# Attention denominators: eight key tiles summed by pair sums on GpSimd and accumulating DMAs, in place of four-tile sums split between GpSimd and TensorE

## The chip, the core and the metric

The kernel runs on one core of a Trainium2 chip. The metric is the device time of one execution in microseconds (us). TensorE multiplies matrices (PE; its weight loads are PEld), VectorE is DVE, ScalarE is ACT, GpSimd is POOL, and SyncE (SP) issues most DMAs.

## What is computed

One transformer block with a conditioned LayerNorm, in float32, over x of 2 x 2048 x 512 with 16 heads of 32 columns:

```python
c6 = silu(c) @ Wc + bc                       # shifts, scales and gates
xm = modulate(ln(x), sh_msa, sc_msa)
q, k, v = xm @ Wq + bq, xm @ Wk + bk, xm @ Wv + bv
w = softmax(einsum('bqhc,bkhc->bhqk', q / DH, k))
y = einsum('bhqk,bkhc->bqhc', w, v)
x = x + g_msa * (y @ Wo + bo)
x = x + g_mlp * (gelu(modulate(ln(x), sh_mlp, sc_mlp) @ W1 + b1) @ W2 + b2)
```

The softmax divides each query's sum of exp(score) * v by the sum of exp(score) over 2048 keys. The change touches only how that denominator is added up.

## The kernel before

Three stages run one after the other: `project`, `attend` (from L646) and `feed_forward`. The change lies in `attend`.

An iteration of `attend` handles 512 queries of one batch and of a group of four heads; there are 32 (`N_IT`). It walks over 16 tiles of 128 keys, and two tiles make a block, so there are 8 blocks in an iteration. For each tile and head, TensorE computes a score tile of 128 keys x 512 queries (`scores`, L1016), and ScalarE turns it into `probs` (exp, L902). Between two score products TensorE computes one product of the next iteration's scores the other way round (L999), whose maximum VectorE takes (`maximum`, L921). These maxima become a row that goes by DMA into the next iteration's query tile (`max_transpose` L1005, `as_row` L931, `load_row` L738). After each block TensorE multiplies the block before by v (`times_v`, L1026), four heads side by side in 32 columns each.

`probs` is a ring of five tiles (`RING`). A tile's slot is written again only when v was multiplied and the tile's sums were read (`slot_free`, L884).

The denominators are built by fours of tiles, here called quads: 128 of them, four in an iteration. GpSimd adds tile to tile: for two of the four heads it adds all four tiles up (`high_first` L812, then `high_more` L819 twice); for the other two heads it adds only tiles 0+1 and 2+3 (`low` L804, twice). That makes five GpSimd instructions of 128 x 1024 for a quad. TensorE then sums over the 128 keys of the partitions with a matrix of ones (`sums`, L1032), due after every second block (`due_quad`). As the halves of neighbouring quads are arranged, an even quad takes 4 of these matmuls and an odd one 8. ScalarE copies each result out of PSUM (`take_sum`, L850). Four heads' matmuls of 32 columns run side by side and are called a group below. In the last iteration VectorE does the `low` sums (`last_low`, L959), as it has no maxima left.

The four sums of an iteration go to `d_small` by small DMAs (L862), are added and inverted on VectorE (L938, L942), go to DRAM and come back broadcast over the partitions (L868, L874), and GpSimd multiplies `y_buf` by them (L825). The result is stored (L882). All of this happens in the iteration behind.

The banks of the maxima and of the sums come from one ring of four PSUM banks, dealt out in advance by `MaxRing`. Every engine runs its queue in order; GpSimd's, too: a wait there holds up all the sums behind it.

Of the kernel before, what the change touches and what calls it, by code (L numbers as in the profile page):

```python
# [11 lines left out]
P = 128  # L12
# [27 lines left out]
RING = 5  # L40
LEAD, BEFORE = 12, 3
# [571 lines left out]
def due_quad(b):  # L613

    return (b - 3) // 2 if b >= 3 and b % 2 == 1 else None


class MaxRing:
# [4 lines left out]
    def __init__(self):  # L623
        uses = []
        for i in range(N_IT):
            for s in range(N_MAX):
# [6 lines left out]
                if within == 2 * HPG - 1 and due_quad(b) is not None and due_quad(b) <= LAST_QUAD:  # L633
                    uses.append(("sum", due_quad(b)))
# [11 lines left out]
def attend(nc, sh, late, x, Wo, W1):  # L646
# [7 lines left out]
    with ExitStack() as ctx:  # L654
# [20 lines left out]
        d_raw, inv = sb("d_raw", [P, QPI, TOK]), sb("inv", [P, TOK])  # L675

        d_small, d_total = sb("d_small", [P, QPI, HPG * TOK // P]), sb("d_total", [P, HPG * TOK // P])
# [15 lines left out]
        low_ready, high_step, last_low_ready = sem("low_ready"), sem("high_step"), sem("last_low_ready")  # L693
# [8 lines left out]
        def low_heads(c):  # L702
            return slice(0, 2) if c % 2 == 0 else slice(2, 4)

        def high_heads(c):
            return slice(2, 4) if c % 2 == 0 else slice(0, 2)

        def lows(c, n):
            return (low_ready, 2 * c + n) if c < LAST_QUAD else (last_low_ready, 2 * (c - LAST_QUAD) + n)

        def low_slot_free(c, half):

            return c - 1 + half if c % 2 == 0 else c - 1
# [4 lines left out]
        def _(sp):  # L718
# [71 lines left out]
        def _(pool):  # L790
# [7 lines left out]
            def low(c, half):  # L798
                first = 4 * c + 2 * half
                hs = low_heads(c)  # L800
                if c >= 2:
                    pool.wait_ge(d_done, low_slot_free(c, half))
                pool.wait_ge(p_done, HPG * (first + 1) + hs.stop)
                pool.tensor_tensor(low_sum[:, (2 * c + half) % 4, :, :], probs[:, first % RING, hs, :],  # L804
                                   probs[:, (first + 1) % RING, hs, :], ALU.add).then_inc(low_ready, 1)

            def high_first(c):
                hs = high_heads(c)
                if c >= 2:
                    pool.wait_ge(d_done, c - 1)  # L810
# [708 lines left out]
```

## Time and profile before

| | us |
|---|---|
| median of 3 runs | 2892.97 (2891.18 to 2893.5) |
| the profiled execution | 2893.33 |
| its span in the trace | 2891.2 |
| PE busy in the span | 2827.3 (98%) |
| POOL busy | 2001.4 (69%) |
| DVE busy | 1995.1 (69%) |
| ACT busy | 1375.4 (48%) |

The shares are averages over the three stages. The attention loop takes some 1,690 us of the span, and each engine must be read in it alone. Matmuls overlap, so a matmul's duration is longer than the distance to the next one's start; what TensorE takes for a piece of work is read from the starts.

### The profile page before, as it was taken

What the parts mean: (1) busy time and instruction counts of PE and PEld (TensorE: products, weight loads), DVE (VectorE), ACT (ScalarE), POOL (GpSimd) and SP (SyncE); (2) the same over time, 40 slices, a digit from 0 to 9 for tenths busy, and PEclk for the clock granted to TensorE, in tenths of its full rate; (3) what the DMA queues carried; (4) which work ended last, traced back from release to release, by engine and by line L of the source; (5) the groups of instructions that cost most, each with busy time, mean ns of one, the idle gap of its engine ahead of it and who ended that gap; (6) DMA issues with size and microseconds to landing.
All of it is one profiled execution on the core that took longest, in us unless ns stands there. A gap on an engine that the chain in (4) does not pass through costs nothing. (4 is left out here: it accounts for less than half of the span.)

```text
span 2891.2 us, 40767 instructions
## 1 busy us (share of the span) xinstructions
PE 2827.3 (98%) x14713; PEld 1811.5 (63%) x14713; DVE 1995.1 (69%) x3320; ACT 1375.4 (48%) x2599; POOL 2001.4 (69%) x1015
## 2 busy tenths in 40 slices
PE   7999999999999999999999999999699999999998
PEld 5777755555555555555555555553488888888887
DVE  5556677777777777777777777773657656666754
ACT  2322266666666666666666666666311211221211
POOL 1000099999999999999999999997555555555453
PEclk9999999999999999999999999999799999999999
DMA  6555533414314314323323324302201101100000
GB/s 233 193 185 172 170 86 82 110 32 103 89 34 100 89 44 101 81 63 87 75 67 89 84 61 94 77 20 100 95 15 44 44 1 44 44 16 29 30 15 15
DMA packets 152767, 225.19 MB, mean 78 GB/s; under 512 B 31804, under 2 KB 48760, under 8 KB 152568
## 3 DMA queue, kind: packets, MB, share of 16 engines
q1 hardware_dynamic: 123036, 204.81, 25.9%
q10 hardware_dynamic: 29532, 17.79, 2.1%
q8 instruction: 118, 1.93, 0.3%
q14 instruction: 81, 0.66, 0.1%
HBM read 162.30 MB, written 58.97 MB: 77 GB/s over the span
## 5 line engine op out<-in xcount | busy, mean ns | idle before, releaser
L921 DVE TENSOR_REDUCE part_max<-m_bank 128x1 f32<-128x512 f32 x1972 | 1207.5, 681 | 385.2 <-PE m_bank L999 385.1
L902 ACT ACTIVATE probs<-s_bank 128x512 f32<-128x512 f32 x2048 | 1035.3, 626 | 196.4 <-PE s_bank L1016 192.3
L804 POOL TENSOR_TENSOR low_sum<-probs 128x1024 f32<-128x1024 f32 x248 | 588.4, 2382 | 80.4 <-ACT probs L902 80.3
L819 POOL TENSOR_TENSOR high_sum<-high_sum,probs 128x1024 f32<-128x1024 f32 x256 | 608.6, 2378 | 40.6 <-ACT probs L902 3.8
L1026 PE MATMUL y_bank<-probs,vs 128*32 128x512 f32 x4096 | 495.6, 602 | 0.0
L1395 ACT ACTIVATE h<-up_bank,vecs 128x512 f32<-128x512 f32 x128 | 88.0, 688 | 574.7 <-PE up_bank L1423 574.7
L1016 PE MATMUL s_bank<-qs,ks 97*128 97x512 f32 x768 | 317.9, 417 | 1.8 <-ACT probs L902 1.5
L1016 PE MATMUL s_bank<-late_parts,ks 97*128 97x512 f32 x768 | 319.0, 416 | 0.2 <-ACT probs L902 0.2
L812 POOL TENSOR_TENSOR high_sum<-probs 128x1024 f32<-128x1024 f32 x128 | 307.5, 2402 | 13.6 <-ACT probs L902 13.3
L1026 PEld LDWEIGHTS y_bank<-probs,vs 128*32 128x32 f32 x4096 | 107.3, 109 | 243.3 <-issue 134.3
L1016 PEld LDWEIGHTS s_bank<-qs,ks 97*128 97x128 f32 x768 | 144.4, 189 | 133.0 <-issue 78.0
L850 ACT ACTIVATE d_raw<-m_bank 128x512 f32<-128x512 f32 x124 | 74.2, 598 | 322.3 <-PE m_bank L1032 322.3
L1016 PEld LDWEIGHTS s_bank<-late_parts,ks 97*128 97x128 f32 x768 | 144.6, 188 | 123.2 <-issue 80.5
L1209 POOL TENSOR_TENSOR w_lo<-space_plain,w_hi 128x512 fp32r<-128x512 f32 x64 | 88.1, 1377 | 179.4 <-DVE w_hi L1291 179.4
L1421 PE MATMUL up_bank<-xm_hi,w_hi 128*128 128x512 f32 x512 | 206.4, 403 | 2.8 <-DVE xm_lo L1287 2.8
L1301 DVE CAST h_hi<-h 128x512 fp32r<-128x512 f32 x128 | 74.4, 582 | 190.5 <-ACT h L1395 190.5
L1423 PE MATMUL up_bank<-xm_hi,w_lo 128*128 128x512 f32 x512 | 203.6, 398 | 0.0
L1422 PE MATMUL up_bank<-xm_lo,w_hi 128*128 128x512 f32 x512 | 203.3, 397 | 0.0
L1422 PE MATMUL acc_bank<-w_lo,h_hi 128*128 128x512 f32 x512 | 202.5, 396 | 0.0
L999 PE MATMUL m_bank<-late_parts 96*128 96x512 f32 x512 | 202.5, 395 | 0.0
L1421 PE MATMUL acc_bank<-w_hi,h_hi 128*128 128x512 f32 x512 | 202.3, 395 | 0.1
L1423 PE MATMUL acc_bank<-w_hi,h_lo 128*128 128x512 f32 x512 | 202.3, 395 | 0.0
(167 smaller groups left out, 4689.3 us busy)
## 6 DMA issues: line engine op xcount, KB each, us to landing
late_parts<-q_parts SPq DMA_DIRECT2D x96, 256.0 KB, 4.8
late_parts<-k_parts SPq DMA_DIRECT2D x72, 256.0 KB, 4.6
ks<-k_parts SPq DMA_DIRECT2D x72, 256.0 KB, 5.0
late_plain<-in_x SPq DMA_DIRECT2D x16, 1024.0 KB, 7.5
q_parts<-qk_out SPq DMA_DIRECT2D x32, 512.0 KB, 3.5
k_parts<-qk_out SPq DMA_DIRECT2D x32, 512.0 KB, 3.5
space_parts<-q_parts SPq DMA_DIRECT2D x48, 256.0 KB, 5.0
space_parts<-k_parts SPq DMA_DIRECT2D x48, 256.0 KB, 4.5
```

The source lines that it names most:

```text
L804: pool.tensor_tensor(low_sum[:, (2 * c + half) % 4, :, :], probs[:, first % RING, hs, :], probs[:, (first + 1) % RING, hs, :], ALU.add).th ...
L812: pool.tensor_tensor(high_sum[:, c % 2, :, :], probs[:, 4 * c % RING, hs, :], probs[:, (4 * c + 1) % RING, hs, :], ALU.add).then_inc(high_ ...
L819: pool.tensor_tensor(high_sum[:, c % 2, :, :], high_sum[:, c % 2, :, :], probs[:, (4 * c + r) % RING, hs, :], ALU.add).then_inc(high_step, 1)
L902: act.activation(probs[:, tile % RING, h, :], s_bank[(HPG * tile + h) % 3][:, :], ACT.Exp).then_inc(p_done, 1)
L921: v.tensor_reduce(part_max[:, i % 2, hs, c:c + 1], m_bank[ring.bank["max", i, n]][:, :], AX.X, ALU.max).then_inc(m_taken, 1)
L999: pe.matmul(m_bank[ring.bank["max", i, n]][:, :], qm[i % 2][0:STACK, h, s * P:(s + 1) * P], km[c][0:STACK, h, :], start=True, stop=True).t ...
L1016: pe.matmul(s_bank[n % 3][:, :], ks[c][0:STACK + 1, h, s * P:(s + 1) * P], qs[i % 2][0:STACK + 1, h, :], start=True, stop=True).then_inc(s ...
L1026: last = pe.matmul(y_bank[h * DH:(h + 1) * DH, :], vs[:, t, h * DH:(h + 1) * DH], probs[:, tile % RING, h, :], start=(t == 0), stop=(t == ...
L1209: pool.tensor_tensor(w1_lo[:, j % 2, :, :], w1_raw[j * 4 // MT][:, :, j % (MT // 4) * P:(j % (MT // 4) + 1) * P], w1_hi[:, j % 2, :, :].bi ...
L1421: pe.matmul(bank, hi_l, hi_r, start=first, stop=False)
L1422: pe.matmul(bank, hi_l, lo_r, start=False, stop=False)
L1423: return pe.matmul(bank, lo_l, hi_r, start=False, stop=last)
```

## The change

Sums are made over eight tiles, here called a half (two halves an iteration). In a quad, GpSimd adds tiles 0+1 into `first_home(c)` and 2+3 into `second_home(c)`, for all four heads in two instructions of 128 x 1024 each. Then GpSimd issues a DMA that adds the second (1 MB) onto the first (`fold_quad`), and after each two quads one that adds one quad onto the other (`fold_half`, 1 MB). TensorE takes 4 matmuls for a half, due after every fourth block, the fifth behind the block that holds the half's last tiles. `fold_half` waits on GpSimd's queue for the DMA of the quad just before; it stands behind the next quad's `first_pair`. `second_pair` waits for the fold two quads back, and the even quads' `first_pair` for TensorE's sums of two halves back. The last four quads are not folded: TensorE takes 8 matmuls for each.

`Wo` is loaded in the last iteration, since its place serves as the second buffer. The denominators' way (move, invert, store, load, multiply, store) is spread over two iterations with two `y_buf` buffers, two moves in place of four, and other places in the queues of ScalarE, VectorE and GpSimd. The last but one iteration's result is finished after the last one's tiles. The size of the memory for GpSimd's DMA descriptors is set to 1024.

```diff
-def due_quad(b):
-
-    return (b - 3) // 2 if b >= 3 and b % 2 == 1 else None
+def due_sum(b):
+
+
+
+
+
+    if b >= N_BLOCKS - 3:
+        return LAST_HALF + b - (N_BLOCKS - 3)
+    return (b - 8) // 4 if b >= 8 and b % 4 == 0 else None
...
-        low_sum = sb("low_sum", [P, 4, 2, TOK])
-        high_sum = sb("high_sum", [P, 2, 2, TOK])
+        first_sum = sb("first_sum", [P, 4, HPG, TOK])
+        second_sum = [sb("second_sum", [P, HPG, TOK]), late.wo]
         part_max, neg_max, neg_max_row = late.part_max, late.neg_max, late.neg_max_row
-        y_buf = sb("y_buf", [P, TOK])
...
+        def first_home(c):
+            return first_sum[:, (0, 1, 2, 0)[c - LAST_QUAD] if c >= LAST_QUAD else c % 4, :, :]
+
+        def second_home(c):
+            if c >= LAST_QUAD:
+                return (second_sum[0][:, :, :], first_sum[:, 3, :, :], second_sum[0][:, :, :], first_sum[:, 1, :, :])[c - LAST_QUAD]
+            return second_sum[c % 2][:, :, :]
+
+        def firsts(c):
+            return (first_ready, 2 * c + 2) if c < LAST_QUAD else (last_first_ready, 2 * (c - LAST_QUAD) + 2)
+
+        def quad_done(c):
+            return quad_folded[c % 2], 16 * (c // 2 + 1)
...
-            sp.dma_start(late.wo[:, :, :], Wo.rearrange("(t p) n -> p t n", p=P)).then_inc(wo_in, 16)
             for i in range(N_IT - 1):
                 iteration(i)
+
+            sp.wait_ge(*quad_done(LAST_QUAD - 1))
+            sp.dma_start(late.wo[:, :, :], Wo.rearrange("(t p) n -> p t n", p=P)).then_inc(wo_in, 16)
...
+            def first_pair(c):
+                h = c // 2
+                if h >= 2 and c % 2 == 0:
+                    pool.wait_ge(d_done, h - 1)
+                if h >= 2 and c % 2 == 1:
+                    pool.wait_ge(half_folded, 16 * (h - 1))
+                for hs in PAIR:
+                    pool.wait_ge(p_done, HPG * (4 * c + 1) + hs.stop)
+                    pool.tensor_tensor(first_home(c)[:, hs, :], probs[:, 4 * c % RING, hs, :],
+                                       probs[:, (4 * c + 1) % RING, hs, :], ALU.add).then_inc(first_ready, 1)
+
+            def second_pair(c):
+                q = c - LAST_QUAD
+                if q == 1:
+                    pool.wait_ge(half_folded, 16 * LAST_HALF)
+                elif q > 1:
+                    pool.wait_ge(d_done, LAST_HALF + q - 1)
+                elif c >= 2:
+                    pool.wait_ge(*quad_done(c - 2))
+                for hs in PAIR:
+                    pool.wait_ge(p_done, HPG * (4 * c + 3) + hs.stop)
+                    pool.tensor_tensor(second_home(c)[:, hs, :], probs[:, (4 * c + 2) % RING, hs, :],
+                                       probs[:, (4 * c + 3) % RING, hs, :], ALU.add).then_inc(second_ready, 1)
+
+            def accumulate(onto, what):
+                return pool.dma_start(onto.rearrange("p h n -> p (h n)"), what.rearrange("p h n -> p (h n)"), accum_op=ALU.add)
+
+            def fold_quad(c):
+                pool.wait_ge(first_ready, 2 * c + 2)
+                pool.wait_ge(second_ready, 2 * c + 2)
+                accumulate(first_home(c), second_home(c)).then_inc(quad_folded[c % 2], 16)
+
+            def fold_half(h):
+                pool.wait_ge(*quad_done(2 * h))
+                pool.wait_ge(*quad_done(2 * h + 1))
+                accumulate(first_home(2 * h), first_home(2 * h + 1)).then_inc(half_folded, 16)
...
+                if c % QPI == QPI - 2 and c // QPI >= 2:
+                    normalise(c // QPI - 2)
                 if c < LAST_QUAD:
-                    low(c, 0)
-                high_first(c)
-                high_more(c, 2)
-                high_more(c, 3)
+                    first_pair(c)
+                if c % 2 == 0 and 0 < c <= LAST_QUAD:
+                    fold_half(c // 2 - 1)
+                second_pair(c)
                 if c < LAST_QUAD:
-                    low(c, 1)
+                    fold_quad(c)
+            normalise(N_IT - 2)
...
+                if i >= 2:
+                    act.wait_ge(y_stored, 16 * (i - 1))
...
                 act.wait_ge(av_done, tile + 1)
-                if r != 1:
-                    act.wait_ge(*lows(c, 1 + r // 2))
-                    act.wait_ge(high_step, 3 * c + max(r, 1))
+                if r == 0:
+                    act.wait_ge(*firsts(c))
+                if r == 2:
+                    act.wait_ge(second_ready, 2 * c + 2)
 
             for i in range(N_IT):
                 for t in range(NKT):
                     tile = NKT * i + t
                     if t == 2 and i:
                         take_y(i - 1)
-                    if tile >= 8 and tile % 4 == 0 and (tile - 8) // 4 < LAST_QUAD:
-                        take_sum((tile - 8) // 4)
+                    if tile >= 18 and tile % 8 == 2 and (tile - 18) // 8 < LAST_HALF:
+                        take_sum((tile - 18) // 8)
...
+                    if i >= 2:
+                        if t == 1:
+                            store_inv(i - 2)
                         if t == 5:
-                            move_sums(i - 1)
-                        if t == 8:
-                            store_inv(i - 1)
-                        if t == 10:
-                            load_inv(i - 1)
-                        if t == NKT - 1:
-                            store_y(i - 1)
+                            load_inv(i - 2)
+                        if t == 13:
+                            store_y(i - 2)
+                    if i and t == 11:
+                        move_sums(i - 1)
+            store_inv(N_IT - 2)
             take_y(N_IT - 1)
+            load_inv(N_IT - 2)
             take_last_sums()
+            store_y(N_IT - 2)
...
+            def last_first(q):
+                c = LAST_QUAD + q
+                if q % 2 == 0:
+                    v.wait_ge(d_done, LAST_HALF - 1 + q // 2)
+                elif q == 1:
+                    v.wait_ge(half_folded, 16 * (LAST_HALF - 1))
+                else:
+                    v.wait_ge(d_done, LAST_HALF + 1)
+                for hs in PAIR:
+                    v.wait_ge(p_done, HPG * (4 * c + 1) + hs.stop)
+                    v.tensor_tensor(first_home(c)[:, hs, :], probs[:, 4 * c % RING, hs, :],
+                                    probs[:, (4 * c + 1) % RING, hs, :], ALU.add).then_inc(last_first_ready, 1)
...
+                        if i and n == INVERT_AT:
+                            invert_small(i - 1)
+            invert_small(N_IT - 3)
...
+            def sums(u):
+                if u <= LAST_HALF:
+                    bank_free(("sum", u))
+                if u < LAST_HALF:
+                    pe.wait_ge(half_folded, 16 * (u + 1))
+                    for h in range(HPG):
+                        last = add_up(u, h, first_home(2 * u)[:, h, :], True, True)
                 else:
+                    c = LAST_QUAD + u - LAST_HALF
+                    pe.wait_ge(*firsts(c))
+                    for h in range(HPG):
+                        add_up(u, h, first_home(c)[:, h, :], c == LAST_QUAD, False)
+                    pe.wait_ge(second_ready, 2 * c + 2)
+                    for h in range(HPG):
+                        last = add_up(u, h, second_home(c)[:, h, :], False, c == N_QUADS - 1)
```

## Rows read from the trace of the kernel before

**Rows 1.** Profile page: the span; busy us, share of the span and instructions.

```profile
span 2891.2 us, 40767 instructions
...
PE 2827.3 (98%) x14713; PEld 1811.5 (63%) x14713; DVE 1995.1 (69%) x3320; ACT 1375.4 (48%) x2599; POOL 2001.4 (69%) x1015
```

**Rows 2.** Windows: each engine's busy us (instructions), TensorE clock, DMA share, GB/s.

```profile
440.00:1990.00 1550.00, 1544.93 (x9013) 830.72 (x9011) 1162.72 (x1985) 1031.18 (x2044) 1435.27 (x622) 1.00 0.32 78
1990.00:2046.00 56.00, 40.34 (x205) 13.29 (x206) 23.90 (x16) 29.20 (x56) 28.38 (x13) 0.84 0.15 51
```

**Rows 3.** Timeline of PE: start, duration, engine, line, operation, tiles, count.

```profile
1201.18 1.92 PE L1026 MATMUL y_bank<-probs,vs 128*32 128x512 f32 x16
...
1208.73 1.92 PE L1026 MATMUL y_bank<-probs,vs 128*32 128x512 f32 x16
...
1214.57 1.92 PE L1026 MATMUL y_bank<-probs,vs 128*32 128x512 f32 x16
...
1221.25 1.92 PE L1026 MATMUL y_bank<-probs,vs 128*32 128x512 f32 x16
...
1253.56 1.92 PE L1026 MATMUL y_bank<-probs,vs 128*32 128x512 f32 x16
```

**Rows 4.** Line L1032, whole span: duration ns min/median/max, first and last start.

```profile
L1032 PE MATMUL m_bank<-low_sum,ones x1024: 592/592/821, 378.0 to 2030.7; 128*32 128x512 f32 x171
...
L1032 PE MATMUL m_bank<-high_sum,ones x512: 592/592/593, 378.0 to 2030.7; 128*32 128x512 f32 x171
```

**Rows 5.** Waits of the weight loads, attention loop: us in total, times, longest.

```profile
PEld y_bank L1026 <- ACT probs L902: 105.2, 331, 0.7
...
PEld m_bank L1032 <- DVE part_max L921: 26.9, 90, 0.3
```

**Rows 6.** Timeline of GpSimd.

```profile
1233.72 1.27 POOL L825 TENSOR_TENSOR y_buf<-y_buf,inv 128x512 f32<-128x512 f32 x1
...
1240.45 4.91 POOL L819 TENSOR_TENSOR high_sum<-high_sum,probs 128x1024 f32<-128x1024 f32 x2
1245.32 4.72 POOL L804 TENSOR_TENSOR low_sum<-probs 128x1024 f32<-128x1024 f32 x2
```

**Rows 7.** Timeline of VectorE: the maxima of one block.

```profile
1205.51 4.88 DVE L921 TENSOR_REDUCE part_max<-m_bank 128x1 f32<-128x512 f32 x8 [2.65 <-PE m_bank L999]
```

**Rows 8.** Timeline of ScalarE: the exps of one block.

```profile
1197.85 4.02 ACT L902 ACTIVATE probs<-s_bank 128x512 f32<-128x512 f32 x8
```

**Rows 9.** Page: DMA queue: packets, MB, share of 16 engines over the span.

```profile
q1 hardware_dynamic: 123036, 204.81, 25.9%
```

**Rows 10.** DMA issues, 2300 to 2800 us: count, KB, median us to landing.

```profile
out<-late_plain SPq DMA_DIRECT2D x16, 256.0 KB, 2.1
late_plain<-in_x SPq DMA_DIRECT2D x4, 1024.0 KB, 5.2
```

**Rows 11.** DMA issues, whole span: a load sent behind others.

```profile
wo<-in_L_cond_Wo SPq DMA_DIRECT2D x1, 1024.0 KB, 14.4
```

**Rows 12.** The issue times on SP's queue, ns, of 1,024 KB loads.

```profile
L1170 SPq DMA_DIRECT2D late_plain<-in_x x6: 390/391/391, 2191.2 to 2703.3; - x6
...
L1156 SPq DMA_DIRECT2D late_plain<-in_x x1: 2152/2152/2152, 2041.9 to 2041.9; - x1
```

**Rows 13.** Timeline, all engines: the maxima's row on its way to the next iteration.

```profile
1236.24 0.51 SPq L738 DMA_DIRECT2D qs<-neg_max_row  x1
...
1243.79 0.50 PE L1016 MATMUL s_bank<-qs,late_parts 97*128 97x512 f32 x1
```

**Rows 14.** Landing times of the row's DMA, whole span.

```profile
DMA to landing us min/median/max: 1.8/2.1/3.5
```

**Rows 15.** Timeline, all engines: the end of the attention stage.

```profile
2025.38 0.67 ACT L902 ACTIVATE probs<-s_bank 128x512 f32<-128x512 f32 x1
...
2031.33 0.60 ACT L855 ACTIVATE d_raw<-m_bank 128x512 f32<-128x512 f32 x1 [1.12 <-PE m_bank L1032]
...
2036.18 0.33 ACTq L882 DMA_DIRECT2D y_cols<-y_buf  x1
```

More of the change, by code:

```diff
@@ L40 @@
 RING = 5
+HALF_QUADS = 2
+LAST_HALF = LAST_QUAD // HALF_QUADS
+HPI = QPI // HALF_QUADS
 LEAD, BEFORE = 12, 3
@@ L632, in __init__ @@
                 b, within = divmod(N_SC * i + s, 2 * HPG)
-                if within == 2 * HPG - 1 and due_quad(b) is not None and due_quad(b) <= LAST_QUAD:
-                    uses.append(("sum", due_quad(b)))
+                if within == 2 * HPG - 1 and due_sum(b) is not None and due_sum(b) <= LAST_HALF:
+                    uses.append(("sum", due_sum(b)))
         self.bank, self.count, self.free_after = {}, {}, {}
@@ L796, in _ @@
             pool.wait_ge(ones_row, BPB - 1)
[L798 to L805, printed above, removed]
@@ L881, in store_y @@
                     act.wait_ge(last_normed, 1)
[L882 removed]
+                act.dma_start(sh.y_cols[group, :, tok:tok + TOK], y_buf[:, i % 2, :]).then_inc(y_stored, 16)
             def slot_free(tile):
@@ L964, in _ @@
                     maximum(i + 1, n)
-                    if i and n == INVERT_AT:
-                        invert_small(i - 1)
                 negative(i + 1)
@@ L974, in _ @@
                         maximum(i + 2, n)
+                        if i and n == INVERT_AT:
+                            invert_small(i - 1)
+            invert_small(N_IT - 3)
             for q in range(QPI):
-                for half in range(2):
-                    last_low(LAST_QUAD + q, half)
-                if q == 1:
+                last_first(q)
+                if q == 2:
                     invert_small(N_IT - 2)
@@ L1028, in times_v, with add_up @@
                 last.then_inc(av_done, 1)
[L1030 to L1031 removed]
+            def add_up(u, h, part, start, stop):
+                bank = m_bank[ring.bank["sum", min(u, LAST_HALF)]]
                 return pe.matmul(bank[h * DH:(h + 1) * DH, :], sh.ones[:, 0:DH], part, start=start, stop=stop)
[L1034 to L1054 removed]
+            def sums(u):
[5 more added lines that the diff above has]
+                        last = add_up(u, h, first_home(2 * u)[:, h, :], True, True)
+                else:
+                    c = LAST_QUAD + u - LAST_HALF
[5 more added lines that the diff above has]
+                        last = add_up(u, h, second_home(c)[:, h, :], False, c == N_QUADS - 1)
                 last.then_inc(d_done, 1)
@@ L1077, in _ @@
                             times_v(2 * b - 1)
-                        if due_quad(b) is not None:
-                            sums(due_quad(b))
+                        if due_sum(b) is not None:
+                            sums(due_sum(b))
             times_v(N_TILES - 2)
             times_v(N_TILES - 1)
-            sums(N_QUADS - 1)
+            sums(LAST_HALF + QPI - 1)
 def feed_forward(nc, sh, late, x, W2, out):
```

101 lines of the change are left out of this document (25 added, 76 removed).

## The prediction

> **What bounds the kernel now.** I read the page first: TensorE is busy for 98% of the span [rows 1]. That is a mean over three stages, so the attention loop comes next, by windows: of 1,550 us TensorE is busy for 1,544.9, GpSimd for 1,435.3 (93%), VectorE for 1,162.7, ScalarE for 1,031.2, at a granted clock of 1.00 [rows 2]. So TensorE sets the pace and GpSimd is close behind; the reader should see that the second number is as important as the first for this change. A busy TensorE may still be waiting, since its ends are modelled; the waits of its weight loads say that in 1,620 us all waits for ScalarE's exps before the y products are 105 us in 331 pieces, at most 0.7 us each, and those for VectorE's maxima before the sums 27 us [rows 5]. They are weight loads that run ahead, beside matmuls. The timeline then gives the unit: the y products of one block start 7.55 us after those of the block before (1201.18 to 1208.73) where an odd quad was summed between them, 5.84 us where nothing was, 6.68 us where an even one was [rows 3]. The even quad costs 0.84 us for its one group of four matmuls, the odd one 1.71 us for its two: 0.85 us a group. An iteration is the distance over eight blocks, 1253.56 - 1201.18 = 52.38 us [rows 3].
>
> **TensorE: groups removed.** The line of the sums has 1,024 + 512 = 1,536 records [rows 4]; 128 quads with 4 and 8 matmuls in turn are 768 matmuls, so each has two records, and there are 192 groups. After the change there are 62 halves of one group and four last quads of two: 70. So 122 groups go, 122 x 0.85 = 103.7 us. In a full iteration six groups become two: 52.38 - 3.40 = 48.98 us, 24.49 us a half. The base is the profiled execution: 2893.33 us, its span 2891.2 and 2.1 around it; the median 2892.97 is the same within 0.4.
>
> **Does another compute engine come first?** VectorE takes a block's eight maxima in 4.88 us [rows 7] and ScalarE its eight exps in 4.02 us [rows 8], against 5.84 us for a block without sums. Such blocks run at full pace already [rows 3], and from now on three of four are such. In an iteration VectorE has 8 x 4.88 = 39.0 us plus some small work, ScalarE 32.2 us plus fewer copies than now, of 48.98. Neither comes first. No cost.
>
> **GpSimd: its work.** Five additions of 128 x 1024 a quad become four. Two additions straight from probs take 4.72 us back to back, those in place 4.91 [rows 6]. A half needs eight, 4 x 4.72 = 18.9 us; half a multiplication of y is 0.64 us (1.27 [rows 6] once in an iteration). New are three DMA issues on GpSimd's queue a half. No DMA is issued from GpSimd in the trace. The nearest rows are SP's issues of 1,024 KB: 0.39 us, and once 2.15 us [rows 12]; I take 1.0, nearer to the usual one, and keep both. With three it is 18.9 + 0.6 + 3.0 = 22.5 us of 24.49: hidden. At 2.15 it is 26.0 us, 1.5 over, and 62 x 1.5 = 93 us of the gain would be gone.
>
> **GpSimd: its wait, the new risk.** `fold_half` waits on GpSimd's queue until the fold of the quad just before has landed. One addition pair of the next quad lies between. Behind it are queued `second_pair`, the next folds, and through them the ring's slots, ScalarE's exps and TensorE. Let L be the time from the issue of a fold to its landing. From that issue to the same one a half later, GpSimd must do in order: L (which covers one pair), three pairs (3 x 4.72 = 14.2), the issue of the half's fold and of the even quad's fold (2.0), half a multiplication (0.6). So a half can't be shorter than L + 16.8 us. Against 24.49, L may be 7.7 us at no cost; each further us costs 62 us in all; against the 26.19 of now (half of 52.38) the change loses from L = 9.4 us on. The ring evens out single delays only, not this mean.
>
> **What is L?** No accumulating DMA is in the trace. A 1,024 KB load that runs alone lands in 5.2 us [rows 10]; this is the low end. An accumulate has to read the destination too. The SP queue's packets took 25.9% of 2891.2 us for 204.81 MB [rows 9], 3.66 us of all 16 engines a MB, 3.8 us for 1,024 KB; with a second reading in full, 5.2 + 3.8 = 9.0 us. A load sent behind others took 14.4 us [rows 11]; this is the far end, for a fold that meets SP's loads. A fold goes from row to row inside the chip's own memory in rows of 8 KB, and the loop's DMA share is 0.32 [rows 2], so I take it nearest to the lone load, between it and the doubled reading: 7.1 us, 0.6 below the 7.7 of above. So the wait is hidden in the forecast, with little to spare.
>
> The Trainium skill (DMA: Bandwidth & Descriptors, Anatomy of one DMA — SWDGE (gpsimd) path) fits a DMA issued from GpSimd by 2.0 us + bytes / 436e3: an estimate of 4.4 us for 1 MiB, and of 6.8 us if 2 MiB are read. By that rule the fold stays hidden in either case, and the time is that of the forecast. The trace has no DMA of this kind to set beside it; its lone load of 5.2 us is 0.8 above the rule.
>
> **The other waits.** `fold_half` is issued some 12 us behind the half's last tiles and TensorE wants it after five blocks, 29 us: 17 us for it to land, free at every L up to the far end. The even `first_pair` waits for sums issued in the same block, which starts it some 3.6 us later than its probs; its slot is wanted about 8 us after that start, against 4.72 of work: free. The row of maxima is issued at 1236.24 and its first user starts at 1243.79 [rows 13], 7.55 us, of which 2.1 (at most 3.5) are landing [rows 14]. The sum after the last block goes, so 6.7 us remain; it is free unless the folds slow it threefold. Two y buffers, fewer moves and the later places of the inverses touch no wait that TensorE has now: nothing from nought to 1 us.
>
> **The end.** Now the last exp starts at 2025.38, the last sums are copied at 2031.33 and y is stored at 2036.18 [rows 15]. GpSimd's last two additions follow heads 2 and 4, so the second ends about 4 us behind the last exp; TensorE fills this with y and the first four matmuls: the last sums come out alike within 1 us. New is that the last but one y is multiplied and stored only here (a load, 1.3 us, a store), just ahead of the last store. I take +2 us, between 0 and +5.
>
> **The sum.** -103.7 + 2 = -101.7, so 2893.33 - 101.7, and from the median the same: 2791 us.
>
> **The rivals.**
> (a) The fold is slower than the cover, but not by much: L between 8 and 9.3 (or an issue near 2.15 us, or a late row). At 9.0 a half is 25.8 us, 1.3 over 24.49: 62 x 1.3 = 81 us back, 2872 us. For it: the doubled reading. Against: large rows, a DMA share of a third.
> (b) The other side, and the strongest: GpSimd's wait for its own fold takes the place of the groups. Place: `fold_half` in GpSimd's queue, every half; it decides from L = 9.4. At 10.5 us a half is 27.3, 2.8 over: 62 x 2.8 = 174 back, 2965 us; at 14.4 it is 31.2, and 3207. For it: GpSimd was at 93% [rows 2], its slack was the kernel's second limit, and half of the loads' time falls beside the folds. Against: the lone load's 5.2 us.
> (c) The 16 DMA engines become the bound. Six folds an iteration at twice 3.8 us are 46 us, and now the share is 0.32 of 52.38, 16.8 us: 62.8 us an iteration, 10.4 over now, 31 x 10.4 = +322, 3215 us. If a fold takes 3.8 us only, the sum is 39.8, and it fits. The packets of now are 2 KB mostly, those of a fold may be larger and so cheaper; this speaks against it.
> The Trainium skill (the same page, Issuing engines are not separate DMA queues) says that DMAs of all queues run on the same 16 engines and interleave; by that rule SP's loads lengthen every fold beside them, which is how (b) and (c) would come about, and it speaks against this change.
> (d) That the change removes what cost nothing: excluded for the groups, since blocks with them are longer by 0.84 and 1.71 us [rows 3].
>
> **How the numbers follow.** Forecast (all hidden, 2784 to 2812): 46%. (a), 2812 to 2887: 17%. Within 0.2%, which is about what a measurement of this kernel can tell from no change, 2887 to 2899: 4%. (b): 26%. (c): 7%. Faster 63%, same 4%, slower 33%. The range goes from 2784 (a shade more than the sum, no cost at the end) up to 2985, where L is about 10.8 us; above it lie (c) and about 8 points of (b), below it 3 points. The forecast's own range is 2784 to 2812.
>
> **What would show it.** Right: iterations of 49.0 us by the y products' starts; blocks of 5.8 us with one in four 0.85 longer; 560 records on the line of the sums; fold landings below 7.7 us; GpSimd busy near 20 us of 24.5 beside its issues. Wrong: gaps on GpSimd in front of the half's fold, ended by a DMA; exps that wait for the ring's slots; a TensorE that waits for ScalarE at every second tile; a DMA share near 0.9; GpSimd's issues above 1.6 us each. The forecast fails first by L, next by the issue time.

## The result and the profile after

The changed kernel takes 2949.97 us (2946.97 to 2954.86), beside 2892.19 us of the kernel before on the same chips: 1.0201 times as long, with a 95% interval from 1.0183 to 1.0219. It is 58 us slower, where 102 us less was forecast. It lies inside the stated range of 2784 to 2985, on the side of rival (b).

The page of the changed kernel: span, busy time, the clock in 40 slices, and the three folds with their median time from issue to landing (the fold of an odd quad reads `wo`, that of an even one `second_sum`):

```profile
span 2950.9 us, 38105 instructions
...
PE 2772.5 (94%) x13737; PEld 1798.9 (61%) x13737; DVE 1992.3 (68%) x3320; ACT 1355.8 (46%) x2537; POOL 1862.3 (63%) x1073
...
PEclk9999999999999999899999999999899999999999
...
first_sum<-second_sum POOLq DMA_DIRECT2D x62, 1024.0 KB, 10.7
first_sum<-wo POOLq DMA_DIRECT2D x62, 1024.0 KB, 8.5
first_sum<-first_sum POOLq DMA_DIRECT2D x62, 1024.0 KB, 9.2
```

TensorE is busy for 55 us less than in [rows 1], so the work did go. It stands still instead, and the clock has a slice at 8 in the middle of the loop. The loop's window shows the same beside [rows 2]: PE 1,435 us of 1,550 (was 1,545), granted clock 0.96 (was 1.00), DMA share 0.90 (was 0.32).

```profile
440.00:1990.00 1550.00, 1434.96 (x7739) 789.24 (x7739) 1128.59 (x1927) 968.04 (x1898) 1255.42 (x652) 0.96 0.90 188
```

The iterations can be read from the transposes of the maxima, one in each: 31 of them, first and last start. Here it is (2023.3 - 391.2) / 30 = 54.40 us an iteration; the same line of the kernel before gives 52.37, in accord with [rows 3].

```profile
L1044 PE MATMUL m_bank<-ident,neg_max x31: 276/277/278, 391.2 to 2023.3; 128*16 128x128 f32 x31
```

**The first stall: GpSimd's wait for its own fold.** GpSimd's timeline in one half:

```profile
1169.39 0.87 POOL L838 DMA_DIRECT2D first_sum<-wo  x1 [0.62 <-POOL wo L834]
1170.00 5.02 POOL L821 TENSOR_TENSOR first_sum<-probs 128x1024 f32<-128x1024 f32 x2
1181.33 0.87 POOL L838 DMA_DIRECT2D first_sum<-first_sum  x1 [6.31 <-ACT probs L932]
1181.94 4.96 POOL L834 TENSOR_TENSOR second_sum<-probs 128x1024 f32<-128x1024 f32 x2
1187.51 0.88 POOL L838 DMA_DIRECT2D first_sum<-second_sum  x1 [0.61 <-POOL second_sum L834]
```

The odd quad's fold is issued at 1169.39. One pair of additions covers it until 1175.0, then GpSimd stands still for 6.3 us until the fold has landed, and only then issues the half's fold (1181.33) and adds the next pair, until 1186.9. The other engines in these microseconds:

```profile
1182.97 0.40 PE L1055 MATMUL s_bank<-qs,ks 97*128 97x512 f32 x1
...
1187.01 2.08 ACT L932 ACTIVATE probs<-s_bank 128x512 f32<-128x512 f32 x4 [4.35 <-POOL second_sum L834]
...
1187.66 0.80 PE L1055 MATMUL s_bank<-qs,ks 97*128 97x512 f32 x1 [4.05 <-ACT probs L932]
...
1188.82 3.64 PE L1065 MATMUL y_bank<-probs,vs 128*32 128x512 f32 x16
```

ScalarE's exps wait for that pair (4.35 us), because it frees the ring's slot; TensorE's score product waits for ScalarE (4.05 us). Behind the gap TensorE's granted clock is down at its lower level, 1.2 GHz: the 16 records of the y products take 3.64 us in place of 1.92 [rows 3]. The waits of the loop (us in total, times, longest) show this chain from end to end:

```profile
POOL first_sum L838 <- ACT probs L932: 174.1, 79, 8.3
...
PEld s_bank L1055 <- ACT probs L932: 116.3, 67, 6.5
...
ACT probs L932 <- POOL second_sum L834: 91.3, 29, 6.3
...
POOL first_sum L838 <- DMA first_sum<-wo: 46.6, 11, 8.1
```

Of GpSimd's waits at its folds 174 us are put down to ScalarE and 47 to the DMA; but the instruction of 1181.33 has only the two quads' folds to wait for. So the two rows are read together, 221 us from 440 to 2,040 us.

From the issue of an odd quad's fold to that of the half's fold it takes 10.2 us in the mean of 56 halves between 440 and 1,990 us (7.5 to 15.7), and from there to the next odd quad's fold 17.2 us (17.0 to 17.6, so without a wait of any size). That the two add up to an iteration, 2 x (10.2 + 17.2) = 54.8 beside the measured 54.40, would be so whatever sets the pace, and proves nothing. What shows that GpSimd's queue sets it is when the half's fold is issued: by the trace's landing times the odd quad's fold lands after 9.5 us in the mean of these halves, and in 55 of the 56 the half's fold follows 0.6 to 0.8 us behind that landing. In these it is the landing, and nothing else, that the half's fold waited for.

**The second stall: a late row.** The row of maxima lands after 6.7 us at the median, and up to 13.0, where it was 2.1 and at most 3.5 [rows 14]:

```profile
DMA to landing us min/median/max: 2.7/6.7/13.0
```

At the change of a group of heads it costs most. The row is issued (1212.57) behind a load of v, and other loads; the next iteration's first score starts only at 1225.67, though TensorE was done with the y products at 1217.9. Then the score products run at a distance of 0.85 us (0.47 at the full clock), until the clock is back:

```profile
1212.15 0.38 SPq L740 DMA_DIRECT2D vs<-v_rows  x1
...
1212.57 1.21 SPq L751 DMA_DIRECT2D late_parts<-neg_max_row  x1
...
1215.96 1.92 PE L1065 MATMUL y_bank<-probs,vs 128*32 128x512 f32 x16
...
1225.67 0.77 PE L1055 MATMUL s_bank<-late_parts 97*128 97x512 f32 x1 [7.79 <-issue]
...
1226.66 0.63 PE L1055 MATMUL s_bank<-late_parts 97*128 97x512 f32 x1
...
1227.51 0.63 PE L1055 MATMUL s_bank<-late_parts 97*128 97x512 f32 x1
```

In the loop from 440 to 2000 us there are 41 gaps of more than 0.3 us in TensorE's timeline, 108.8 us together: 85 us in front of exps that were late, 24 us put down to no engine, at the iterations' starts. In the loop the clock is down for 126 us, of which 29 us lie inside such gaps; before, for none.

### The profile page after: what moved, and what is told of

Its sections match the earlier page's. It is cut to its first block and busy times, and to the rows that moved or that the text cites. A ratio compares the mean times of both kernels' runs of the same rounds, so it can differ in the third digit from the quotient of the medians.

```text
span 2950.9 us, 38105 instructions
## 1 busy us (share of the span) xinstructions
PE 2772.5 (94%) x13737; PEld 1798.9 (61%) x13737; DVE 1992.3 (68%) x3320; ACT 1355.8 (46%) x2537; POOL 1862.3 (63%) x1073
## 5 line engine op out<-in xcount | busy, mean ns | idle before, releaser
L821 POOL TENSOR_TENSOR first_sum<-probs 128x1024 f32<-128x1024 f32 x248 | 617.1, 2636 | 26.6 <-PE m_bank L1071 26.4
L1065 PE MATMUL y_bank<-probs,vs 128*32 128x512 f32 x4096 | 520.7, 628 | 0.0
L834 POOL TENSOR_TENSOR second_sum<-probs 128x1024 f32<-128x1024 f32 x128 | 320.7, 2668 | 3.8 <-PE m_bank L1071 3.8
L834 POOL TENSOR_TENSOR wo<-probs 128x1024 f32<-128x1024 f32 x124 | 310.0, 2641 | 0.0
L1038 PE MATMUL m_bank<-space_parts,late_parts 96*128 96x512 f32 x500 | 203.4, 407 | 1.3
```

The lines of the kernel that those rows point to most:

```text
L821: pool.tensor_tensor(first_home(c)[:, hs, :], probs[:, 4 * c % RING, hs, :], probs[:, (4 * c + 1) % RING, hs, :], ALU.add).then_inc(first_ ...
L834: pool.tensor_tensor(second_home(c)[:, hs, :], probs[:, (4 * c + 2) % RING, hs, :], probs[:, (4 * c + 3) % RING, hs, :], ALU.add).then_inc ...
L1038: pe.matmul(m_bank[ring.bank["max", i, n]][:, :], qm[i % 2][0:STACK, h, s * P:(s + 1) * P], km[c][0:STACK, h, :], start=True, stop=True).t ...
L1065: last = pe.matmul(y_bank[h * DH:(h + 1) * DH, :], vs[:, t, h * DH:(h + 1) * DH], probs[:, tile % RING, h, :], start=(t == 0), stop=(t == ...
```

## The experiments

Two theories first, then a third. A: the order of GpSimd's queue, that is its wait for the quad's fold with one pair as cover. B: the 16 DMA engines are full, with 5.3 us for each fold. C: the late row.

Each kernel was timed beside the kernel before, which took 2893.88 us (e1 to e4), 2893.95 us (e5 to e8) and 2890.98 us (e9, e10).

**e4: no folds at all.**

```diff
-                if c % 2 == 0 and 0 < c <= LAST_QUAD:
-                    fold_half(c // 2 - 1)
                 second_pair(c)
-                if c < LAST_QUAD:
-                    fold_quad(c)
...
-                    pe.wait_ge(half_folded, 16 * (u + 1))
+                    pe.wait_ge(first_ready, 4 * u + 4)
```

> The changed kernel without its folds: neither DMAs nor waits for them; the sums take only the first pair of each eight tiles. It measures what TensorE's removed groups are worth alone. By the sum of the prediction 2784 to 2795. If the freed time of TensorE came back as a wait for VectorE or ScalarE, it would be above 2830.

Measured: 2779.14 us, ratio 0.9605 (0.9591 to 0.962), 5 us below what was expected. All that the change takes off TensorE is worth 114.7 us, 0.94 us for each of the 122 groups; the forecast had 0.85. By the starts of the y products a block with a group is only 0.88 us longer here (6.66 against 5.78), which makes 107 us; where the other 7 come from is open. An iteration is (1854.5 - 393.7) / 30 = 48.69 us:

```profile
L1034 PE MATMUL m_bank<-ident,neg_max x31: 276/278/278, 393.7 to 1854.5; 128*16 128x128 f32 x31
```

This kernel's attention stage ends near 1,911 us, so its loop is read up to 1,850: PE is busy for 1,407 of 1,410 us, with a clock of 1.00 and a DMA share of 0.35. Neither VectorE nor ScalarE took the freed time, and the inverses' longer way costs nothing that can be seen.

```profile
440.00:1850.00 1410.00, 1407.25 (x7910) 794.64 (x7912) 1149.44 (x1971) 982.17 (x1942) 1133.10 (x493) 1.00 0.35 81
```

**e2: folds of a quarter.**

```diff
-                return pool.dma_start(onto.rearrange("p h n -> p (h n)"), what.rearrange("p h n -> p (h n)"), accum_op=ALU.add)
+                return pool.dma_start(onto[:, 0, :], what[:, 0, :], accum_op=ALU.add)
```

> The changed kernel, but each fold adds only the first head's quarter (256 KB in place of 1,024 KB); the other three heads' sums lack what isn't folded. Waits, issues and additions stay. If landing time and traffic are what costs (theories A and B, and C by contention), landings fall to 3 to 5 us, the DMA share to about 0.5 and the time to 2788 to 2805. If GpSimd's issues and longer additions cost by themselves, it stays above 2850.

Measured: 2779.28 us, 0.9614 (0.9597 to 0.963), the same as without folds, and 9 us below the least that was expected. The three issues a half (0.88 us each), their waits and GpSimd's additions are therefore hidden; only what depends on the folds' bytes costs. The landings are 3.4 to 4.7 us by the medians, and here the half's fold is issued 3.4 us (median) behind the odd quad's landing, not 0.6: GpSimd no longer waits for its own fold.

**e3: plain copies.**

```diff
-                return pool.dma_start(onto.rearrange("p h n -> p (h n)"), what.rearrange("p h n -> p (h n)"), accum_op=ALU.add)
+                return pool.dma_start(onto.rearrange("p h n -> p (h n)"), what.rearrange("p h n -> p (h n)"))
```

> The changed kernel with each fold a plain copy of the same 1,024 KB from the same queue (the destination is overwritten, so the sums lack the tiles that would have been added). It measures what accumulating costs over copying. If the destination's reading doubles the work of the DMA engines, as my high end had it, the landing falls from 8.5 us to about 5 and the DMA share from 0.90 to 0.6 to 0.7, and the time to 2790 to 2830. If a copy is no cheaper, landing and time stay at 8.5 us and 2950.

Measured: 2796.97 us, 0.9659 (0.9639 to 0.968). The folds' queue from 500 to 1900 us (packets, MB, share of 16 engines), first in the changed kernel, then with copies:

```profile
q0 software_dynamic: 21994, 160.13, 57.7%
```

```profile
q0 software_dynamic: 24484, 178.29, 38.0%
```

An accumulated MB takes 0.577 x 1400 / 160.13 = 5.0 us of all engines, a copied one 0.380 x 1400 / 178.29 = 3.0 us: 1.7 times as much for the same bytes, not twice, as my high end had it. For 1,024 KB these are 5.3 and 3.1 us. The landings of all folds, in the changed kernel and with copies:

```profile
DMA to landing us min/median/max: 6.9/9.4/14.2
```

```profile
DMA to landing us min/median/max: 4.4/6.1/13.3
```

The least is 6.9 us against 4.4, the median 9.4 against 6.1.

**e1: the half's fold later.**

```diff
-                if c % 2 == 0 and 0 < c <= LAST_QUAD:
-                    fold_half(c // 2 - 1)
                 second_pair(c)
+                if c % 2 == 0 and 0 < c <= LAST_QUAD:
+                    fold_half(c // 2 - 1)
```

> The changed kernel with one thing moved: the half's fold is issued behind the even quad's second pair of additions in place of in front of it. No traffic, no issue and no addition less. Theory A (order: GpSimd stands still at the half's fold until the quad's fold has landed, 8.5 us median, at most 14.2, with only one addition pair of 5.0 us in between): with two pairs in between GpSimd can cover 10 to 11 us and more, the waits of the exps for GpSimd's second pair (91 us in the loop of the changed kernel) go, and the time falls to 2800 to 2850. Theory B (the 16 DMA engines, busy for 0.90 of the loop, are the bound): moving a wait gives back nothing lasting, 2910 to 2950. Theory C (the late row of maxima costs the most): 2900 to 2940, with the gaps at the iterations' starts as they are.

Measured: 2936.82 us, 1.0149 (1.0134 to 1.0164): 13 us back, of some 170. Theory A alone fell. The edit did more than lengthen the cover: the half's fold and the even quad's fold are now issued 0.65 us apart, where they were 6.2, and each fold lands later still (12.9 us at the median of all, up to 20.7; 9.4 and 14.2 before the edit):

```profile
first_sum<-second_sum POOLq DMA_DIRECT2D x62, 1024.0 KB, 15.9
first_sum<-wo POOLq DMA_DIRECT2D x62, 1024.0 KB, 12.5
first_sum<-first_sum POOLq DMA_DIRECT2D x62, 1024.0 KB, 10.4
```

The DMA share is 0.90, as in the changed kernel, and the waits have moved on. TensorE's sums wait for the half's fold, 36.6 us in 17 pieces, which didn't occur in the changed kernel. The larger part is the row: it now lands up to 21.9 us after its issue, and the gaps at the iterations' starts, 24 us in the changed kernel, are 62 us in 9 pieces.

```profile
440.00:1990.00 1550.00, 1431.53 (x7812) 805.38 (x7811) 1141.91 (x1949) 977.72 (x1918) 1263.80 (x659) 0.96 0.90 189
```

```profile
PE s_bank L1055 <- issue: 62.2, 9, 16.7
PE m_bank L1071 <- DMA first_sum<-first_sum: 36.6, 17, 3.8
```

**e6: the row from ScalarE's queue.**

```diff
-                if i + 1 < N_IT:
-                    load_row(i + 1)
...
+                    if t == 13 and i + 1 < N_IT:
+                        load_row(i + 1)
```

> The changed kernel with the DMA of the row of maxima issued from ScalarE's queue at tile 13 in place of SyncE's, so that it isn't queued behind 1 MB of key and value loads. Folds and traffic stay. C (late row): the gaps at the iterations' starts go (24 us in the changed kernel's loop, and with them part of its 126 us at half the clock), 2905 to 2925. If the row is late only because the engines are full (B), it stays at 2940 to 2950.

Measured: 2940.16 us, 1.0166 (1.0149 to 1.0183): 10 us back, less than C wanted and at the edge of what B said. The gaps at the iterations' starts are gone but for 4 us, and no landing of the row is above 9.2 us; but the exps' waits for GpSimd are as long as before the edit (92 us, were 91), and so, nearly, are GpSimd's at its folds (116.5 + 105.7 = 222 us, 218 in the changed kernel over the same stretch; only the share put down to the fold has grown). The first stall is untouched:

```profile
POOL first_sum L836 <- ACT probs L935: 116.5, 66, 7.2
POOL first_sum L836 <- DMA first_sum<-wo: 105.7, 21, 9.1
...
ACT probs L935 <- POOL second_sum L832: 92.1, 26, 7.3
```

**e7: light loads.**

```diff
+def load_head(sp, dst, src, parts, group, tok, done):
+    for r, part in enumerate(parts):
+        sp.dma_start(dst[r * DH:(r + 1) * DH, 0:1, :].bitcast(F32),
...
-                load_stacked(sp, ks[c], sh.k_parts, K_PARTS, group, c * TOK, ks_in[c])
+                (load_head if group else load_stacked)(sp, ks[c], sh.k_parts, K_PARTS, group, c * TOK, ks_in[c])
```

The same goes for `km`, `qm` and `qs`.

> The changed kernel, but SyncE's reloads of keys and queries in the attention loop bring only one head in four (the other heads keep what they had, so the results are not the attention's). Folds, waits, issues and order stay. B (the DMA engines are full of folds and loads together, and a fold is late because of the loads beside it): fold landings fall from 8.5 to about 7 us, the DMA share to about 0.7, and the time to 2780 to 2810. A (the cover is too short even for a lone fold): a lone fold lands in 6.9 us, the smallest landing seen, so a remainder of waits would stay only if the cover is below that: above 2830.

Measured: 2832.34 us, 0.9788 (0.9774 to 0.9803): 118 us less than the changed kernel, with every fold in place. The odd quad's fold lands after 7.2 us at the median, as B said, and the share is 0.75 in the loop, read up to 1,850 us. But 53 us against e4 remain, more than B had: an iteration is (1899.5 - 393.3) / 30 = 50.21 us.

```profile
first_sum<-wo POOLq DMA_DIRECT2D x59, 1024.0 KB, 7.2
```

```profile
L1050 PE MATMUL m_bank<-ident,neg_max x31: 276/277/278, 393.3 to 1899.5; 128*16 128x128 f32 x31
```

```profile
440.00:1850.00 1410.00, 1384.23 (x7655) 763.82 (x7653) 1113.69 (x1909) 959.76 (x1882) 1241.97 (x645) 1.00 0.75 158
```

By GpSimd's timeline, from the odd quad's fold to the half's fold it is 8.0 us in the mean of 59 halves (7.5 to 10.1), and 17.2 from there on. In 58 of the 59 the half's fold follows the landing within 0.8 us. This is theory A's cycle again, now with a landing of 7.3 us in the mean, and it still sets the pace: the landing is longer than its cover of one pair.

The folds' own work is the same as with full loads. Their queue from 500 to 1900 us:

```profile
q0 software_dynamic: 23972, 174.50, 63.1%
```

That is 0.631 x 1400 / 174.50 = 5.1 us of all engines a MB, against 5.0 in the changed kernel. A fold beside full loads lands later without being more work, which fits a wait behind the loads' packets. The loads' reading of DRAM became less by the same edit; that it has no part in this is not shown.

**e10: light loads, the half's fold later and the row from ScalarE.** The edits of e1, e6 and e7 together.

> Both edits, and SyncE's reloads of keys and queries bring one head in four (the others keep what they had, so the results are not the attention's). With light loads alone the iteration was 50.2 us, and GpSimd's cycle of L = 7.2 us explains 50.6. Here that cycle is cut: if it was all that remained, 48.7 us an iteration and 2779 to 2790 us. If accumulating itself slows something else (GpSimd's additions take 5.0 us a pair beside folds and 4.7 without), it stays above 2810.

Measured: 2794.62 us, 0.9666 (0.9651 to 0.968); (1866.5 - 393.7) / 30 = 49.09 us an iteration.

```profile
L1055 PE MATMUL m_bank<-ident,neg_max x31: 276/277/278, 393.7 to 1866.5; 128*16 128x128 f32 x31
```

With the loads light, the edits of e1 and e6 are together worth 35 us (0.9788 to 0.9666 of the kernel before); with full loads they are worth 26 (e9). So the order is a limit of its own, and here it is gone: the half's fold is issued 3.9 us (mean) behind the odd quad's landing and never within 0.9, so GpSimd no longer waits for its own fold, and the time is within 18 us of the kernel without folds. The 5 us above the expectation stay open; GpSimd's additions start 4.7 us a pair apart here as everywhere, so they are not the cause.

**e9: both edits, full loads.**

> The changed kernel with both edits: the half's fold behind the even quad's second pair, and the row of maxima issued from ScalarE. The result is complete, the traffic unchanged. GpSimd's cycle of waits is then not the limit, and the row isn't behind the loads. If the row's lateness (65 us or so of gaps put down to no engine in the kernel with the half's fold later) hid the gain of the order (A and C together), 2830 to 2870. If the DMA engines are full by themselves (B: 48.5 us of all 16 engines' time an iteration against 48.7 us of TensorE), the folds only land later still and the sums wait for them: 2900 to 2935.

Measured: 2923.69 us, 1.0111 (1.0082 to 1.0141), in B's range; the eight runs spread from 2898 to 2936. The kernel is still 33 us slower than before the change and 129 us slower than e10, which has the same order and the same queue for the row, but light loads. Neither stall is gone: the odd quad's fold now lands after 12.3 us in the mean, longer than its cover of two pairs, and in 33 of 58 halves the half's fold still follows that landing within 0.8 us; the row lands up to 14.5 us after its issue. The window and the folds' landings:

```profile
440.00:1990.00 1550.00, 1451.29 (x7904) 804.09 (x7903) 1152.73 (x1968) 986.43 (x1938) 1278.06 (x667) 0.96 0.92 191
```

```profile
first_sum<-first_sum POOLq DMA_DIRECT2D x58, 1024.0 KB, 10.9
first_sum<-second_sum POOLq DMA_DIRECT2D x58, 1024.0 KB, 16.7
first_sum<-wo POOLq DMA_DIRECT2D x58, 1024.0 KB, 13.0
```

**e5: one level of folds.** Quads are folded by DMA, the half's fold is left out, and TensorE sums both quads of a half.

```diff
-                if c % 2 == 0 and 0 < c <= LAST_QUAD:
-                    fold_half(c // 2 - 1)
...
-                    pe.wait_ge(half_folded, 16 * (u + 1))
-                    for h in range(HPG):
-                        last = add_up(u, h, first_home(2 * u)[:, h, :], True, True)
+                    pe.wait_ge(*quad_done(2 * u))
+                    pe.wait_ge(*quad_done(2 * u + 1))
+                    for n in range(2):
+                        for h in range(HPG):
+                            last = add_up(u, h, first_home(2 * u + n)[:, h, :], n == 0, n == 1)
```

> One level of folds only: quads are folded by DMA as in the changed kernel, the half's fold is gone, and TensorE sums the two quads of a half (8 matmuls in place of 4). The result is complete. Groups: 62 x 2 + 8 = 132, 60 fewer than before at 0.92 us (the worth of a group by the kernels without folds, 114.7 / 122 = 0.94), and 62 more than the changed kernel. If the DMA engines' load is the cause (B: 5.4 us of all engines a fold, so 6 x 5.4 + 16.8 = 49 of 48.7 us an iteration; now 4 x 5.4 + 16.8 = 38.4 of 50.6), stalls go and it is 2894 - 55 = 2835 to 2845. If the order of GpSimd's queue is the cause (A), the same, since the wait for the quad's fold goes with the half's. If both stay a cost in another place (late row, C), above 2870.

Measured: 2879.77 us, 0.9953 (0.9939 to 0.9968). It is faster than before by 0.5%, less than expected, and in the range that the expectation gave to C. The DMA share is 0.76, the clock 0.99, an iteration (1944.5 - 393.5) / 30 = 51.70 us. The exps' waits for GpSimd are gone; up to the last full iteration the gaps of more than 0.3 us in TensorE's timeline are 28 us, every one at an iteration's start. C, which was small in the changed kernel, is the largest thing that this kernel pays.

```profile
440.00:1990.00 1550.00, 1514.40 (x8601) 831.96 (x8593) 1165.12 (x1987) 1017.14 (x2006) 1264.49 (x621) 0.99 0.76 158
```

```profile
L1042 PE MATMUL m_bank<-ident,neg_max x31: 276/277/278, 393.5 to 1944.5; 128*16 128x128 f32 x31
```

**e8: one level, and the row from ScalarE.** The edits of e5 and e6.

> One level of folds, and the row of maxima issued from ScalarE's queue. The result is complete. If one level has no row gaps left, the same as one level alone, 2835 to 2845; if the late row is what remains of its cost, up to 15 us less.

Measured: 2859.35 us, 0.9881 (0.9864 to 0.9897), 20 us less than e5 where 15 at most were expected. TensorE is busy for 1,529 of 1,550 us, the gaps up to the last full iteration sum to 9 us, and an iteration is (1927.5 - 394.1) / 30 = 51.11 us. This version computes the whole result and beats both kernels, the one before by 1.2%. (The row's DMA also stands at another place in time than in e5, at tile 13; what the queue alone is worth is not separated from that.)

```profile
440.00:1990.00 1550.00, 1528.84 (x8678) 822.30 (x8670) 1168.89 (x1992) 1020.79 (x2018) 1272.79 (x625) 1.00 0.76 158
```

```profile
L1047 PE MATMUL m_bank<-ident,neg_max x31: 276/277/279, 394.1 to 1927.5; 128*16 128x128 f32 x31
```

The kernels in one table; "engines" is the DMA share in the loop times the iteration, in us of all 16 engines. The share is read from 440 to 1,990 us, and for e2, e3, e4, e7 and e10, whose attention stage ends earlier, from 440 to 1,850. The times come from four sets of runs, in which the kernel before lies within 3 us.

| kernel | us | iteration | DMA share | engines |
|---|---|---|---|---|
| before | 2892.2 | 52.37 | 0.32 | 16.8 |
| changed | 2950.0 | 54.40 | 0.90 | 49.0 |
| e6, the row from ScalarE | 2940.2 | 53.94 | 0.90 | 48.5 |
| e1, half's fold later | 2936.8 | 53.92 | 0.90 | 48.5 |
| e9, both | 2923.7 | 53.41 | 0.92 | 49.1 |
| e5, one level | 2879.8 | 51.70 | 0.76 | 39.3 |
| e8, one level and the row | 2859.4 | 51.11 | 0.76 | 38.8 |
| e7, light loads | 2832.3 | 50.21 | 0.75 | 37.7 |
| e3, plain copies | 2797.0 | 49.07 | 0.75 | 36.8 |
| e10, light loads and both | 2794.6 | 49.09 | 0.76 | 37.3 |
| e2, quarter folds | 2779.3 | 48.71 | 0.55 | 26.8 |
| e4, no folds | 2779.1 | 48.69 | 0.35 | 17.0 |

TensorE alone needs 48.7 us an iteration, and the DMA engines have 49 us of work for it; in no kernel were they busy for more than 0.92 of the loop. Wherever the engines' work was cut to 37 to 39 us, by fewer folds, by copies or by lighter loads, the time came nearer to what TensorE needs (48.7 us; in e5 and e8, with two groups more, some 50.5); wherever only the order was changed, it did not.

## Why the prediction was wrong

**What bounds the kernel.** Right, and the second number, GpSimd's 93%, was indeed where it turned.

**TensorE's groups.** Right in kind: the sums' line fell to 560 records, and in e4 nothing took their place. The group was read at 0.85 us and is 0.88 by the starts in e4; with 7 us that no row explains, 114.7 us were won in place of 103.7.

**VectorE, ScalarE.** Right (e4).

**GpSimd's work.** Right that it is hidden (e2). An issue lasts 0.88 us in the records, and the next addition starts 0.6 us after it, but a quad's fold is issued 5.6 us after the start of the pair that it reads, 0.9 later than the next pair would be. Together that is what was put in: the cycle without L was put at 16.8 us and is 17.2. (The records of additions beside folds last longer, 5.0 us a pair; their starts are as far apart as ever, 4.7.)

**The wait.** The step that failed is "so I take it nearest to the lone load", with its 7.1 us, and behind it "So the wait is hidden". The distance that stands for L is 10.2 us in the mean. The formula it went into was right: L + 16.8 against 24.49, with a loss against the kernel before from L = 9.4 on. With 10.2 it gives 27.0 us a half, 2.5 over 24.49, 62 x 2.5 = +155 on 2791, 2946 us; measured were 2950. So rival (b) came true, at the place and nearly at the price it was given. That it fits so closely is partly luck: with the terms as measured, 27.2 us a half (54.40 / 2) against 24.35 (48.69 / 2) on e4's 2779, it is 2956 us.

Of the missing 3.1 us the estimate of a fold by itself has hardly any part: with light loads it lands after 7.3 us in the mean (e7), beside the 7.1. 0.6 to 0.7 us lie between a landing and the next issue on GpSimd's queue, which the sum had at nothing. The other 2.2 us are the loads beside it: 9.5 us in the mean with full loads, 7.3 with light ones. A value for a fold with room was used as the mean of one without.

**The DMA engines.** Rival (c) was priced at 62.8 us of engines' work an iteration, and had 7%. The work is 49.0 us: the doubled reading was too dear for rows of 8 KB (5.3 us a fold, not 7.7), and "it fits", said of 39.8 us at the low price of 3.8, is no proof of no cost: e7, with 37.7, is 53 us slower than e4. At 49.0 against TensorE's 48.7 the engines would have to be busy without a break, and that fits what was seen: moving the wait (e1) or the row (e6), or both (e9), gives back 13, 10 and 26 us and not 170. I treated (b) and (c) as two cases; they are one. L isn't a property of the fold but of what the engines have beside it (7.3 and 9.5 us for the same fold in the same order), and it rose to 12 us when the half's fold was moved and folds lay on top of each other (e1, e9).

That rule of the Trainium skill that spoke against the change (DMA: Bandwidth & Descriptors, Issuing engines are not separate DMA queues) is borne out: SyncE's loads of 256 KB of keys, for one, land after 9.4 us in the changed kernel and 5.0 in that before. Its fit for a DMA issued from GpSimd (the same page, Anatomy of one DMA — SWDGE (gpsimd) path), 4.4 us for 1 MiB, is close to the least landing of a plain copy, 4.4 us; for an accumulate with twice the bytes it gave 6.8, and the least landing is 6.9. So the rule meets the fastest folds, and the mistake was to use such a value as the mean.

**The other waits.** "It is free unless the folds slow it threefold": they did, from 2.1 to 6.7 us, which the text named and left at no cost. In the changed kernel the row has 24 us of gaps for itself, in e1 62; in e5 they are all the gaps that remain. "Free at every L up to the far end" held in the changed kernel for TensorE's wait for the half's fold, no longer in e1.

**The clock.** This term was missing. In the changed kernel's loop every gap of 3 us or more comes with a stretch at 1.2 GHz, which begins in it or just behind it; they sum to 126 us. 29 of them lie inside the gaps, where nothing is lost, and the other 97 cost about half, some 49 us by this estimate. With the 109 us of gaps that is 158 of the 171 us between the changed kernel and e4; the other 13 are not accounted for.

**The end.** Forecast +2 us. From the start of the last exp to the copy of the last sums it is 6.8 us (5.95 in [rows 15]), to the last stores 11.4 (10.8):

```profile
2083.70 0.68 ACT L932 ACTIVATE probs<-s_bank 128x512 f32<-128x512 f32 x1
...
2090.52 0.60 ACT L884 ACTIVATE d_raw<-m_bank 128x512 f32<-128x512 f32 x1 [1.12 <-PE m_bank L1071]
...
2095.11 0.87 ACTq L911 DMA_DIRECT2D y_cols<-y_buf  x2
```

Under 1 us later, inside what was stated.

## What to carry to other kernels

When work moves from a busy engine to DMAs, first sum the DMA engines' time over an iteration (share times length, plus the new bytes at their own price) and compare it with the bound of the iteration; close to it, landing times here weren't those of a lone transfer, and cover that was added was eaten by later landings. Two distances on one queue that add up to the iteration don't show that this queue sets the pace; look whether the waiting instruction starts right behind the event that it waits for. A wait on an in-order queue for a DMA just issued closes a cycle whose length can be added up beforehand, and the landing in it must be the mean under load. Take the step that pays most for its bytes: here one level of folding, with the small urgent DMA on another queue, gave 1.2% (e8), and with the second level the best complete kernel was 1.1% slower than before (e9).

## What the runs showed of the hardware that was not expected

An accumulating DMA of 1,024 KB in rows of 8 KB took 5.3 us of all 16 engines' time and landed after 6.9 us at best; a plain copy of the same bytes 3.1 and 4.4 us. SyncE's 8 KB row, to one partition, went from 2.1 to 6.7 us with the engines at 0.90. A DMA issue on GpSimd's queue takes 0.88 us by its record, and the next instruction starts after 0.6; behind the landing of a DMA that GpSimd's queue waits for, its next issue came after 0.6 us. After a gap of 4 us TensorE's granted clock was down to 1.2 GHz, for 126 us of the loop in all.
